# Earlier stores, loads and late inverses at the seam, and four heads of cross-attention masked by a minimum on VectorE

## The reference, cut to what matters

```
x = x + delta_attention(layernorm(x))          # delta rule in chunks of 32, long and short convolution, gates
x = x + cross_attention(layernorm(x), ctx, mask)
x = x + quantised_ffn(layernorm(x))

# delta rule, per chunk of 32 positions
inv = -(kb @ k.T) * strict_lower
for i in range(1, 32): inv[i] += inv[i] @ inv  # row by row
inv = inv + eye;  u = inv @ v;  w = inv @ kb   # then a recurrence over 8 chunks with state S
local_long = causal_dwconv(v, fir_long)        # 64 taps; used in the gates and in the output

# cross-attention, 16 heads of 16 channels
scores = Q @ K.T / 4
scores = where(mask == 0, -inf, scores)        # the mask leaves out keys at the end, the same for all rows
out = softmax(scores) @ V
```

## Time and profile before

| | |
|---|---|
| time, three runs | 1314.67 us median (1303.68, 1314.67, 1316.67) |
| profiled execution | 1310.53 us, span 1308.7 us, mean granted clock 0.913 |
| busy, share of the span | PE 1081.1 us (83%), DVE 955.4 (73%), ACT 877.0 (67%), POOL 634.1 (48%) |
| DMA | 160.27 MB, 122 GB/s mean, 65320 of 159824 packets under 512 B |
| L1446, mask matmuls of pass B | 256, of 376 to 634 ns |
| L2132, maxima | 248, 170.2 us in all |

### The profile page before, as it was taken

One profiled execution on the slowest core, in us unless ns is written; L12 is line 12 of the kernel. 1 busy time (PEld: TensorE's weight loads), 2 busy tenths in 40 slices (PEclk: granted clock), 3 DMA queues, 4 the chain that ended last, 5 costly groups with the idle time before them and its releaser, 6 DMA issues. The chain is left out here.

```text
span 1308.7 us, 27567 instructions
## 1 busy us (share of the span) xinstructions
PE 1081.1 (83%) x8643; PEld 799.5 (61%) x8643; DVE 955.4 (73%) x2188; ACT 877.0 (67%) x1695; POOL 634.1 (48%) x2360
## 2 busy tenths in 40 slices
PE   5889798664676779999999999999999887875756
PEld 4677676663555556776776677677677644443224
DVE  5998989676666767777877777787787566534985
ACT  5778877332343567878878877887887665444866
POOL 4777775304265355465456546546555643111007
PEclk9988988885667889999999999999999998897989
DMA  6666666454115233433434343343332431204007
GB/s 186 200 211 216 207 201 182 168 125 131 57 57 153 70 86 110 124 112 95 146 108 137 110 127 106 110 146 114 114 126 82 124 95 54 66 34 168 17 1 225
DMA packets 159824, 160.27 MB, mean 122 GB/s; under 512 B 65320, under 2 KB 126656, under 8 KB 159680
## 3 DMA queue, kind: packets, MB, share of 16 engines
q1 hardware_dynamic: 159680, 158.52, 40.5%
HBM read 96.34 MB, written 61.87 MB: 121 GB/s over the span
## 5 line engine op out<-in xcount | busy, mean ns | idle before, releaser
L2132 DVE TENSOR_REDUCE x_maxima<-x_psA 128x2 f32<-128x512 f32 x248 | 170.2, 686 | 93.6 <-PE x_psA L1425 91.3
L1692 ACT ACTIVATE x_psA<-x_mask_q 128x512 f32<-128x512 bf16 x239 | 142.5, 596 | 55.8 <-DVE x_maxima L2132 52.8
L1685 ACT ACTIVATE x_PT<-x_psB 128x512 f32<-128x512 f32 x240 | 143.0, 596 | 54.6 <-PE x_psB L1449 49.9
L314 DVE SCALAR_TENSOR_TENSOR a_conv<-a_ps_proj,taps,a_conv 128x253 f32<-128x253 f32 (+2 forms) x288 | 114.9, 470 | 14.7 <-ACT a_conv L381 14.7
L1425 PE MATMUL x_psA<-x_Ks,x_Qs 96*128 96x256 bf16 x496 | 97.9, 279 | 19.9 <-ACT x_psA L1692 19.3
L537 PE MATMUL a_ps_proj<-a_hT,wqkv 128*128 128x256 f32 x384 | 106.1, 425 | 9.9 <-DVE a_conv L314 6.6
L1446 PE MATMUL x_psB<-x_mask_k,x_ident_bf 128*128 128x512 bf16 x240 | 93.5, 390 | 12.9 <-ACT x_PT L1685 10.6
L537 PEld LDWEIGHTS a_ps_proj<-a_hT,wqkv 128*128 128x128 f32 x384 | 78.7, 216 | 29.4 <-issue 14.6
L1449 PE MATMUL x_psB<-x_Qs,x_Ks 98*128 98x256 bf16 x480 | 93.7, 276 | 0.0
L1853 POOL TENSOR_SCALAR x_parts_q<-x_rest 128x512 bf16<-128x512 f32 x16 | 23.9, 1494 | 114.1 <-DVE x_rest L2108 114.1
L1463 PE MATMUL x_psO<-x_PT,x_V 128*32 128x256 f32 x1024 | 70.8, 395 | 1.0 <-ACT x_PT L1685 1.0
(11 more groups left out here) (387 smaller groups left out, 3231.9 us busy)
## 6 DMA issues: line engine op xcount, KB each, us to landing
scratch_keypack<-a_keypack SPq DMA_DIRECT2D x16, 768.0 KB, 3.6
c_keypack<-scratch_keypack SPq DMA_DIRECT2D x16, 768.0 KB, 4.7
x_Ks<-scratch_k_parts SPq DMA_DIRECT2D x192, 64.0 KB, 2.3
matrix<-scratch_taps_copies SPq DMA_DIRECT2D x32, 256.0 KB, 4.1
scratch_k_parts<-x_parts_k SPq DMA_DIRECT2D x32, 192.0 KB, 2.2
scratch_q_parts<-x_parts_q SPq DMA_DIRECT2D x32, 192.0 KB, 2.2
x_Qs<-scratch_q_parts SPq DMA_DIRECT2D x32, 192.0 KB, 2.9
a_x_in<-in_x SPq DMA_DIRECT2D x16, 256.0 KB, 3.8
```

The costliest lines, as they stand in the source:

```text
L314: nc.vector.scalar_tensor_tensor(acc, ps_proj[PROJ_BANK[p]][:, c, 0:L - j], taps[:, p, c, TAPS - 1 - j:TAPS - j], acc, ALU.mult, ALU.add). ...
L1685: nc.scalar.activation(PT[:, k % (2 * GROUP)], bank_B(b, k)[0], ACT.Exp, scale=XD ** -0.5).then_inc(pexp_ready, 1)
L1692: nc.scalar.activation(psA[:].rearrange("p t q -> p (t q)"), mask_q[:, k % 2].rearrange("p s k -> p (s k)"), ACT.Copy).then_inc(mask_writt ...
L2132: nc.vector.tensor_reduce(maxima[:, t, 2 * pair:2 * pair + 2], bank_A(b, k)[0], AX.X, ALU.max).then_inc(maxed, 1)
```

## The change

It has two parts.

1. **The seam.** Of the four last stores SP issues two and ACT two. `long[0]` is loaded after the first five of SP's loads in place of after all, with its wait on the stores. The transposes of the late triangles move: one behind `att0` (op `invb`), one behind `att1` (op `invs`). POOL's ones and zeros follow at `invb`. The first three steps of the late inverse move from that place to the first `invr`, which runs eight steps now. The transposes back move from the begin of turn 4 to the end of turn 3 (op `inve`), ahead of the maximum `mA0`. `r1` writes into `rv` in place, so the buffer `rhs1` goes, and POOL's `rv` of the next batch waits for the solve's matmul.
2. **The mask.** For heads 2, 6, 10 and 14 pass B has no mask matmul, so the exponential of a masked key is some positive number (at most 1, or more where a masked score lies above the maximum). DVE then sets it to zero: `min(exponential, kept_k)`, 128 x 512, where `kept_k` is 2 for a kept key and 0 for a masked one. The ops are `cl2`, `cl6`, `cl10`, `cl14`; each waits for its head's exponential, and `pv` waits for them. `kept_k` is made once. Both inputs and the output lie in SBUF.

```diff
+            sp.wait_ge(kept, GROUPS // 2)
+            store_long(nc.sync, 0, range(FC))
+            sp.wait_ge(kept, GROUPS)
+            store_long(nc.sync, 1, range(1))
...
+            act.wait_ge(kept, GROUPS)
+            store_long(nc.scalar, 1, range(1, FC))
...
-        LATE_STEPS = {(0, "b"): (1, 4), (1, "r"): (4, 9), (1, "d"): (9, 14), ...
+        LATE_STEPS = {(1, "r"): (1, 9), (1, "d"): (9, 14), ...
...
-            for dst, src in loads:
+            for n, (dst, src) in enumerate(loads):
+                if n == 5:
+                    sp.wait_ge(early["long_stored"], 128)
+                    sp.dma_start(long[0][:], dram["long_tok"][:, :, 0]).then_inc(vs_loaded[0], 16)
                 sp.dma_start(dst, src, allow_slow_non_contiguous=True).then_inc(xw_loaded, 16)
...
-                    nc.tensor.matmul(bank.rearrange("p t q -> p (t q)"), ident_bf[:], mask_k[:].rearrange("p t q -> p (t q)"),
-                                     start=True, stop=False, skip_group_check=True)
+                    if k not in CLEARED:
+                        nc.tensor.matmul(bank.rearrange("p t q -> p (t q)"), ident_bf[:], mask_k[:].rearrange("p t q -> p (t q)"),
+                                         start=True, stop=False, skip_group_check=True)
                     for t in range(TT):
                         last = nc.tensor.matmul(bank[:, t], Ks[slot][:, k, t * P:(t + 1) * P], Qs[slot][:, k],
-                                                start=False, stop=True, skip_group_check=True)
+                                                start=k in CLEARED, stop=True, skip_group_check=True)
...
                     pe.wait_ge(pexp_ready, HEAD_STEPS * b + GROUP * (g + 1))
+                    pe.wait_ge(cleared, len(CLEARED) * b + sum(k < GROUP * (g + 1) for k in CLEARED))
...
-                        pool.wait_ge(rhs1_ready, b)
+                        pool.wait_ge(solve_mm, 6 * (b - 1) + 4)
...
-                    nc.vector.tensor_tensor(rhs1[:], rv[:, 1], ps_w[:, 0:D], ALU.subtract).then_inc(rhs1_ready, 1)
+                    nc.vector.tensor_tensor(rv[:, 1], rv[:, 1], ps_w[:, 0:D], ALU.subtract).then_inc(rhs1_ready, 1)
...
-                    if (b, op) == (0, "inv0"):
-                        for q in range(LATE_GROUPS):
-                            at = (EARLY_GROUPS + q) * CH
-                            nc.vector.transpose(M[:, q].rearrange("p i j -> p (i j)"),
-                                                keep["X32"][:, at:at + CH].rearrange("p s c -> p c s")).then_inc(inverse_step, 1)
+                    if (b, op) in ((0, "invb"), (0, "invs")):
+                        q = ("invb", "invs").index(op)
+                        at = (EARLY_GROUPS + q) * CH
+                        nc.vector.transpose(M[:, q].rearrange("p i j -> p (i j)"),
+                                            keep["X32"][:, at:at + CH].rearrange("p s c -> p c s")).then_inc(inverse_step, 1)
...
-                    elif (b, op) == (4, "inv0"):
+                    elif (b, op) == (3, "inve"):
...
+                elif op[:2] == "cl":
+                    k = int(op[2:])
+                    if b == 0 and k == CLEARED[0]:
+                        dve.wait_ge(mask_k_ready, 1)
+                        nc.vector.tensor_scalar(kept_k[:], mask_k[:], 0.0, 2.0, ALU.is_equal, ALU.mult).then_inc(prep_step, 1)
+                        dve.wait_ge(prep_step, 7)
+                    dve.wait_ge(pexp_ready, HEAD_STEPS * b + k + 1)
+                    pt = PT[:, k % (2 * GROUP)]
+                    nc.vector.tensor_tensor(pt, pt, kept_k[:], ALU.min).then_inc(cleared, 1)
```

More of the change, by code:

```diff
@@ L631, in phase_b, with store_long @@
         block = ctx.enter_context(nc.Block())
+        def store_long(queue, stage, halves):
+            for half in halves:
+                for part in range(2):
+                    at = slice(half * P + stage * HB, half * P + stage * HB + HB)
+                    queue.dma_start(dram["long_tok"][part * HB:part * HB + HB, :, :, at].rearrange("p t b c -> p (t b) c"),
+                                    keep["long"][half * HB:half * HB + HB, part, :, stage * HB:stage * HB + HB]).then_inc(long_stored, 16)
         @block.sync
@@ L777 @@
 NVB = 2
-C_ORDER = [(0, "tt"), (0, "inv0"), (3, "og2"), (3, "oge"), (1, "rv"), (4, "kA1"), (3, "ogs"), (3, "ctxT"), (2, "tT"), (2, "tTc"), (3, "cTc"),
+CLEARED = (2, 6, 10, 14)
+C_ORDER = [(0, "tt"), (3, "og2"), (3, "oge"), (1, "rv"), (4, "kA1"), (3, "ogs"), (3, "ctxT"), (2, "tT"), (2, "tTc"), (3, "cTc"),
            (1, "sums0a"), (1, "sq0"), (7, "rstdb"), (1, "p2"), (1, "xur"), (4, "sA1"), (4, "mA1"), (4, "ld_K1"), (4, "kA2"),
@@ L845, in phase_cx @@
         rv = sb("rv", [P, TT, D])
-        rhs1 = sb("rhs1", [P, D])
         U = sb("U", [P, TT, D])
@@ L947, in phase_cx @@
         LATE_GROUPS = NQ - EARLY_GROUPS
-        inverse_step, upper_cleared = sem("inverse_step"), sem("upper_cleared")
+        inverse_step = sem("inverse_step")
         ALL_STEPS = LATE_GROUPS + CHAIN_STEPS + LATE_GROUPS
-        LATE_STEPS = {(0, "b"): (1, 4), (1, "r"): (4, 9), (1, "d"): (9, 14), (1, "a"): (14, 15), (1, "s"): (15, 16), (2, "p"): (16, 17),
+        LATE_STEPS = {(1, "r"): (1, 9), (1, "d"): (9, 14), (1, "a"): (14, 15), (1, "s"): (15, 16), (2, "p"): (16, 17),
                       (2, "d"): (17, 19), (2, "a"): (19, 21), (3, "k"): (21, 22), (3, "x"): (22, 23), (3, "q"): (23, 25),
@@ L992, in phase_cx @@
         mask_k = xb("mask_k", [P, TT, L], BF16)
+        kept_k = xb("kept_k", [P, TT, L], BF16)
         ident_bf = xb("ident_bf", [P, P], BF16)
@@ L1044, in phase_cx @@
         shift_loaded = [xsem(f"shift_loaded{i}") for i in range(STACKS)]
-        scoreB_mm, pexp_ready = xsem("scoreB_mm"), xsem("pexp_ready")
+        scoreB_mm, pexp_ready, cleared = xsem("scoreB_mm"), xsem("pexp_ready"), xsem("cleared")
         pv_mm, OT_ready = xsem("pv_mm"), xsem("OT_ready")
@@ L1180, in _ @@
                 sp.dma_start(clip[:, 0, n:n + 1], bass.AP(dram[name].tensor, 0, [[0, P], [1, 1]])).then_inc(xw_loaded, 16)
-            sp.wait_ge(early["long_stored"], 128)
-            sp.dma_start(long[0][:], dram["long_tok"][:, :, 0]).then_inc(vs_loaded[0], 16)
             turns(later)
@@ L1233, in part @@
                     g = int(op[-1])
-                    right = rv[:, 0] if g == 0 else rhs1[:]
+                    right = rv[:, g]
                     if g == 0:
@@ L1781, in part @@
                     nc.gpsimd.tensor_scalar(out[3], by_tile(stat_y[:]), 1.0 / H, None, ALU.mult).then_inc(stat_step, 1)
-                elif (b, op) == (0, "inv0"):
+                elif (b, op) == (0, "invb"):
                     for q in range(LATE_GROUPS):
@@ L1787, in part @@
                         for i in range(CH - 1):
-                            last = nc.gpsimd.memset(M[:, q, i, i + 1:CH], 0.0)
-                        last.then_inc(upper_cleared, 1)
+                            nc.gpsimd.memset(M[:, q, i, i + 1:CH], 0.0)
                 elif op == "ostat":
@@ L2087, in part @@
                             nc.vector.tensor_tensor(below, below, out, ALU.add).then_inc(inverse_step, 1)
-                    elif (b, op) == (4, "inv0"):
+                    elif (b, op) == (3, "inve"):
                         dve.wait_ge(inverse_step, LATE_GROUPS + CHAIN_STEPS)
-                        dve.wait_ge(upper_cleared, LATE_GROUPS)
+                        dve.wait_ge(rv_ready, 1)
                         for q in range(LATE_GROUPS):
```

## The result

The changed kernel takes 1339.26 us (median of four runs, 1336.13 to 1341.92) against 1315.67 us before: a ratio of 1.0191, 95% interval 1.0157 to 1.0225. It is slower by 24 to 25 us (the medians lie 23.6 apart, the ratio makes it 25), where 1318 us and no measurable change were forecast; the time lies above the range. The profiled execution took 1336.1 us with a span of 1334.3, 25.6 us more than the span before.

The account below looks back on a forecast made before the run. The prediction took a loop through TensorE's stream, `xnx`, `qrest` and 16.4 us of GpSimd to bound the 46.5 us turn. Seam -9.7 and mask +19 on 1310.5 gave 1319.8, taken as 1318 us; range 1294 to 1331.

Parts of the forecast that it names:

- hidden tenths: Whole sum: the turn may hide some tenths in waits TensorE still has, so 1319.8 became 1318 us.
- .55 at `xnx`: Steady turn: `cl2` and `cl6` delay `xnx`, so `xT` and head 10 come later, +.55 us a turn.
- .9 at GpSimd: Steady turn: `cl10` and `cl14` each hold up GpSimd's chain by .45 us, +.9 a turn.
- the loop: Steady turn: TensorE's stream, `xnx` in the middle, `qrest`, 16.4 us of GpSimd, back to TensorE; work cut elsewhere gives nothing.
- the port: VectorE's two-SBUF-input minima block GpSimd's SBUF reads: .45 us on each chain, 1.3 a turn by the full rule.
- Two turns behind them ... +2; the last two ... -.7: Turns after the first twelve: +2 us for two with weights prepared on VectorE, -.7 for the last two, VectorE idle.
- is met at every group: New wait of `pv`: each minimum is done some matmuls before its four heads are multiplied, so no wait.
- VectorE waits too: Rival, 20%: `cl2` beside GpSimd's `klow` loses another .4 to .5 us; with full blocking the turn is 2.2 longer, 1330 us.
- -9.7 us: Seam: `r1` 10.7 us earlier through earlier gate and `long[0]`, less 1 for moved transposes; ends -6 and -13.
- the gate does not move: Rival, 12%: stores paced by the 16 transfer engines, two queues issue no faster; seam gives 6, time 1322 us.
- TensorE is the bound: Rival, 13%: each mask matmul left out pays, 64 x .21 = 13.6 us, time 1287 us.

Follow-up runs that it names:

- the one with one input: Changed kernel with the minima of heads 10 and 14 replaced by equally long row-maximum reduces with one SBUF input: 1327.67 us, ratio 1.0102.
- head 8's minimum: Part 1 plus head 8 alone without mask matmul, its minimum ahead of head 10's maximum, against the kernel before: 1309.50 us, again 1307.18 us.

## Why the prediction was wrong

The sum was made against the profiled execution, so its 1318 stands against 1336.1, a miss of 18 us: 8.5 in the first phase, 3.7 in the seam, 3.2 in the end, 1.8 taken off for hidden tenths and 1.1 in the turns. By its terms:

- **The turn was right, with luck in one term.** 1.45 us were forecast, .55 at `xnx` and .9 at GpSimd; measured were 1.5: .63 ahead of head 10 and .85 behind it. Twelve turns cost 18.5 us for 17.4. The experiment without minima and the one with one input confirm the loop and the port. But at `xnx` two errors made up for each other: `cl2`, taken at .1, cost .34, and `cl6`, taken at .6, cost .31. The forecast's 1.8 us off the sum for hidden tenths had no row behind it, and was not there.
- **The end failed.** "Two turns behind them ... +2; the last two ... -.7" gave 1.3 us. It was 5 to 12 us in the four kernels with all four minima against the mean of the two profiles of before, 5 in the changed kernel's own; the run with minima for twelve batches has the end of before. I gave these turns the price of a minimum, since VectorE idles there, and wrote that the new wait of `pv` "is met at every group". It is in the steady turns. But in the last three batches `pv3` waits 1.38, 1.52 and 1.09 us for `cl14`, all the time that TensorE waits for a minimum at `pv` in this kernel; the first of these stands in the turn that is longer, and the matmuls behind it run at 1.2 GHz. From `mA0` of batch 15 to the end the changed kernel takes 181.5 us, as before (181.6 and 182.6). The rival 'VectorE waits too' described the wait of 1.63 us at `qlow`; I looked for it at `cl2` in the steady turn, where all minima took .66 to .72, and not in the turns in which it occurs. The kernel with the reduces hasn't this wait, and its end is no shorter.
- **The seam was too large.** -9.7 us were forecast; from the filter's last copy to `mA0` of batch 1 it is -5.9 in this profile, and -6.6 as the mean of two profiles of part 1 against two of before. The gate came 3.6 us earlier (4.1 forecast), but `long[0]` was ready 19.2 us after the filter's last copy and not 16.8: its issue waited for the stores until 306.32, 14.9 us after the copy for the 12.8 that I took from a landing time with one queue. From there VectorE's leg to `r1` took 11.9 us for 11.8, so `r1` came 8.1 us earlier and not 10.7. The rest lies between `r1` and `mA0` of batch 1, a stretch that differs by 3.7 us between the two profiles of the kernel before, so it can't be told from such differences. The rival 'the gate does not move' had the right reason and the wrong place: the gate moves, the data do not. The Trainium skill (DMA: Bandwidth & Descriptors, section Issuing engines are not separate DMA queues), which I named beside that rival, grants a saving of issuing time, and so speaks for the gate to move.
- **The profile of one execution.** 8.5 us of this profile's difference lie in the first phase, ahead of all that the change touches, and nothing in the forecast allowed for it. Without it, the profile has 16.5 us more than the mean of the two profiles of before, while the medians lie 23.6 apart. In the ten other kernels of the experiments the same count lies within 3.5 us of the medians. So either the end costs more in the changed kernel's runs without a profile, as it does in the other kernels with four minima, or not all of the 8.5 us is a draw; that stays open. Of the 21 us between forecast and median, some 5 are the base: 1310.5 lies 5.1 us under the later median of before, and I had named 4 of them and added none.

The rival 'TensorE is the bound' is refuted: without matmul and without minimum the turn falls by .15 us of .86.

## What to carry to other kernels

Before work is moved from an engine with the highest busy share to one that idles, follow the chain that closes a steady turn: here it ran through the layer norm and GpSimd's small instructions, so TensorE's savings became waits, and VectorE's added work was paid ahead of the layer norm and through a port. An instruction with two SBUF inputs on VectorE is placed where GpSimd rests; head 8's minimum at such a place was a small gain, four others a loss of 30 us. Price the first and last turns of a pipeline on their own rows, with each new wait in them, and the range from more than one execution, because a phase that isn't touched can move by more than the effect.

## What the runs showed of the hardware that was not expected

- One phase of the same code, rich in DMA, took between 242.1 and 256.4 us over thirteen profiled executions.
- Two queues for the last four of eight equal stores: the issuing was done 3.6 us earlier, but the last store landed 14.2 to 15.2 us after the filter's last copy in nine profiles, against 13.2 to 14.1 in four profiles with one queue, and the dependent load came no sooner.
- In the turn from batch 14 to 15, where TensorE has gaps, the granted clock was .79 to .86 with one minimum a batch or none, and the turn 45.8 to 48.2 us long; with two reduces and two minima or with four minima it was .69 to .77, and 52.2 to 54.7 us.
